# First two token groups routed inside the first attention, and GpSimd's scatters in fours

## The reference, cut to what matters

```python
x = x + tanh(g_xattn[0]) * L0_xattn(layernorm(x), ctx_1024, mask)      # 375 keys for each batch
h = layernorm(x)
# L0_ffn: mixture of 8 experts, top 2, 1024 places for each expert
probs = softmax(h @ Wr)                       # [3584, 8]
w_topk, e_topk = top_k(probs, 2)
pos = running count of the tokens of the same expert      # in the order of the tokens
buf[e, pos] = h                               # kept while pos < 1024
buf_out = expert_e(rms(buf)) + buf
y = h + sum_k w_topk[k] * buf_out[e_topk[k], pos[k]]      # where both of a token's places were kept
y = gelu(fh @ fWg) * (fh @ fWu) @ fWd + h                 # where one overflowed; fh = rms(h) * f_norm
x = x + tanh(g_ffn[0]) * y
```

## Time and profile before

| | us |
|---|---|
| median of three runs | 3190.02 (3184.22 to 3192.74) |
| profiled execution, first to last instruction | 3224.8 |
| first attention, up to the first instruction of the next block | 209.5 |
| routing stage, up to the last instruction on VectorE | 350.6 |
| busy over the span: TensorE, VectorE, ScalarE, GpSimd | 3044.6, 2015.2, 1460.1, 620.4 |

### The profile page before, as it was taken

The page is one execution under the profiler, slowest core; times in us unless marked ns, Lnnn a source line. Parts: engine busy times, 40 slices in busy tenths (PEclk is TensorE's granted clock), DMA queues, the critical chain, the costliest instruction groups (busy, mean ns, idle before and its releaser), DMA issues. The chain is left out here.

```text
span 3224.8 us, 61178 instructions
## 1 busy us (share of the span) xinstructions
PE 3044.6 (94%) x23544; PEld 2321.0 (72%) x23544; DVE 2015.2 (62%) x4390; ACT 1460.1 (45%) x2835; POOL 620.4 (19%) x895
## 2 busy tenths in 40 slices
PE   8995799997989999999999999799999999899999
PEld 6874456656779999999999999566666666566443
DVE  3454211125767777788787877566666666688654
ACT  3431111114645555555555555366666666455000
POOL 3535200024300013023002300112212111035000
PEclk8987899988999999999999999899999999999999
DMA  8652232236700000000000000000000000245000
GB/s 240 192 169 62 62 118 103 93 113 192 235 25 2 1 2 1 2 2 2 2 1 2 2 1 2 22 24 21 16 21 21 16 21 16 74 147 186 15 15 17
DMA packets 75072, 181.80 MB, mean 56 GB/s; under 512 B 12101, under 2 KB 18738, under 8 KB 74452
## 3 DMA queue, kind: packets, MB, share of 16 engines
q1 hardware_dynamic: 58260, 137.83, 13.5%
q10 hardware_dynamic: 10192, 25.30, 2.5%
q0 software_dynamic: 6336, 14.76, 1.6%
HBM read 150.25 MB, written 27.79 MB: 55 GB/s over the span
## 5 line engine op out<-in xcount | busy, mean ns | idle before, releaser
L2664 ACT ACTIVATE probs<-probs,neg_top 112x375 f32<-112x375 f32 x512 | 281.8, 599 | 12.8 <-DVE neg_top L2587 11.6
L2587 DVE CUSTOM_DVE_ANT_0 probs<-ps,add 112x375 f32<-112x375 f32 x512 | 250.2, 546 | 55.6 <-PE ps L2738 54.7
L3202 PE MATMUL ps<-we,xn_t 128*112 128x512 f32 x512 | 230.5, 614 | 0.9 <-PEq L736 0.9
L2144 DVE TENSOR_REDUCE top<-ps 112x16 f32<-112x1792 f32 x96 | 194.3, 2024 | 58.5 <-PE ps L2382 57.1
L2765 PE MATMUL ps<-ident,probs 112*125 112x112 f32 x1536 | 222.5, 281 | 2.8 <-DVE probs_t L2594 2.8
L2594 DVE COPY probs_t<-ps 125x336 f32<-125x336 f32 x256 | 128.9, 504 | 151.4 <-PE ps L2765 151.4
L1524 DVE TENSOR_TENSOR hidden<-gated,ps 128x512 f32<-128x512 f32 x64 | 44.0, 688 | 284.7 <-PE ps L1567 284.7
L2765 PEld LDWEIGHTS ps<-ident,probs 112*125 112x125 f32 x1536 | 189.7, 188 | 30.7 <-issue 18.9
L2160 DVE TENSOR_TENSOR probs<-probs,inv_sum 112x1792 f32<-112x1792 f32 x96 | 197.4, 2056 | 3.3
L2156 DVE TENSOR_REDUCE row_sum<-probs 112x16 f32<-112x1792 f32 x96 | 193.9, 2020 | 4.3 <-ACT probs L2268 4.3
L2148 DVE TENSOR_TENSOR probs<-ps,top 112x1792 f32<-112x1792 f32 x96 | 194.3, 2024 | 3.3
(11 more groups left out here) (419 smaller groups left out, 6255.2 us busy)
## 6 DMA issues: line engine op xcount, KB each, us to landing
ctx_t<-in_ctx_T_dram SPq DMA_DIRECT2D x96, 375.0 KB, 4.2
ctx_sb<-in_ctx_dram ACTq DMA_DIRECT2D x64, 384.0 KB, 5.7
ctx_sb<-in_ctx_dram SPq DMA_DIRECT2D x32, 384.0 KB, 6.0
ctx_sb<-in_ctx_T_dram SPq DMA_DIRECT2D x32, 375.0 KB, 3.0
queue<-zeros SPq DMA_DIRECT2D x32, 256.0 KB, 4.5
rows<-queue SPq DMA_DIRECT2D x16, 512.0 KB, 5.0
outputs<-out SPq DMA_DIRECT2D x16, 512.0 KB, 2.9
mask_in<-in_mask_BxSxS_fk_dram SPq DMA_DIRECT2D x16, 328.1 KB
```

The source lines that it names most:

```text
L2144: dve.tensor_reduce(top[:, :, :], scores, AX.X, ALU.max).then_inc(s["top_done"], 1)
L2587: dve.tensor_tensor_reduce(out=probs[:, u, h, :], in0=k.ps[0:S, SCORE + h, 0:L], in1=add[:, j % 2, :], scale=1.0, scalar=BIG, op0=ALU.add, ...
L2664: act.activation(probs[:, u, h, :], probs[:, u, h, :], ACT.Exp, bias=neg_top[:, u, h:h + 1], scale=-1.0).then_inc(s["probs_done"], 1)
L3202: mm = pe.matmul(k.ps[0:S, Y + at % YB, :], xn_t[:, j + u, c, :], r.we[:, c, e:e + TWO, :].rearrange("p e d -> p (e d)"), start=c == 0, st ...
```

## The change

The diff rewrites the routing as functions outside of the stages (`token_norm`, `token_shift`, `token_exp`, `token_pick`, `token_places`, `token_rows`, `token_scatter`, `token_gains`, `token_self`), whose bodies do what the functions above did, and calls them from two stages:

- Inside `first_attention`, from step 10 on, one batch is transposed and its logits computed in each step, 24 batches (three groups) in all. Groups 0 and 1 are routed completely: picked in steps 18 and 26, placed in steps 19 and 27, rows found in steps 20 and 28, and scattered two transfers to a step in steps 20 to 35. Group 2 is shifted and picked in step 34. `normalise` for 28 of 32 batches and `add_self` for 16 of them run there too. The block ends when the 32 scatters have landed.
- In `route_tokens` are left: the scales and norms of the last 4 batches, places and rows of group 2, all of group 3 but its first four norms, 32 scatters, and the whole shared branch, which has a new order. After every fourth scatter GpSimd waits until it has landed.
- The writes of zeros go out two to a step from step 5 on, so that all are out after step 20's load.
- The small tiles move into the memory of the network's weights, which is unused until `run_experts`; the scales are computed in halves of a group.

```diff
                     if j == CT:
                         sp.dma_start(k.x_sb[:, BODY:B, :], ...)
-                    else:
-                        sp.dma_start(fill[j - CT - 1], k.zeros[:, :]).then_inc(k.queue_zeroed, 16)
-                for n in range(B - CT - 1, B):
-                    sp.dma_start(fill[n], k.zeros[:, :]).then_inc(k.queue_zeroed, 16)
+                    for n in range(2 * (j - CT - 1), min(2 * (j - CT), k.zero_dmas)):
+                        if j > CT:
+                            sp.dma_start(fill[n], k.zeros[:, :]).then_inc(k.queue_zeroed, 16)
...
+                def scatter(j):                                   # GpSimd, first_attention
+                    g, turn = divmod(j - 20, G)
+                    if j == 20:
+                        pool.wait_ge(k.queue_zeroed, k.zero_dmas * 16)
+                    if 0 <= g < 2:
+                        for n in (2 * turn, 2 * turn + 1):
+                            token_scatter(k, t, pool, g, n)
...
+                token_half_scales(k, m, pool, 6)
+                for j in range(B, B + 4):
+                    pool.wait_ge(s["residual_done"], j - LAG)
+                    scatter(j)
+                for g in range(2):
+                    pool.wait_ge(t.scattered[g], 16 * G * TOP_K)
...
+                    if 0 <= j - TOKENS < ROUTED:                  # TensorE, first_attention
+                        transpose_token(j - TOKENS)
...
+                    if 0 <= j - TOKENS < ROUTED:
+                        token_logits(j - TOKENS)
+                    if 0 <= g < 2 and j == G * g + 19:
+                        token_places(k, m, t, pe, g, PLACES)
...
-                pool.wait_ge(k.queue_zeroed, k.zero_dmas * 16)    # GpSimd, route_tokens
-                for g in range(GROUPS):
-                    pool.wait_ge(s["put_ready"], g + 1)
-                    for j in range(G):
-                        for r in range(TOP_K):
-                            pool.indirect_dma_start(k.queue[:, :], ...).then_inc(scattered[g], 16)
+                token_half_scales(k, w, pool, GH * GROUPS - 1)
+                token_sizes(k, w, pool, LAST)
+                token_inverses(k, w, pool, LAST)
+                for g in (LAST - 1, LAST):
+                    for n in range(G * TOP_K):
+                        token_scatter(k, t, pool, g, n)
+                        if n % 4 == 3:
+                            pool.wait_ge(t.scattered[g], 16 * (n + 1))
...
+                for x in range(B - HB, B):                        # VectorE, route_tokens
+                    token_norm(k, w, t, dve, x)
+                token_rows(k, w, t, dve, LAST - 1, PLACES)
+                token_gains(k, w, t, dve, LAST - 1)
+                hide(0)
+                for x in range(G * (LAST - 1), G * LAST):
+                    token_self(k, t, dve, x)
+                hide(1)
+                token_shift(k, w, t, dve, LAST, LOGITS)
+                add_shared(0)
+                token_pick(k, w, t, dve, LAST)
+                hide(2)
+                add_shared(1)
+                token_rows(k, w, t, dve, LAST, PLACES)
+                hide(3)
+                token_gains(k, w, t, dve, LAST)
+                for x in range(G * LAST, B):
+                    token_self(k, t, dve, x)
+                add_shared(2)
+                hide(4)
+                for n in range(3, GH * GROUPS):
+                    add_shared(n)
+                    if n + 2 < GH * GROUPS:
+                        hide(n + 2)
...
+                token_places(k, w, t, pe, LAST - 1, PLACES)       # TensorE, route_tokens
+                gate_and_up(0)
+                for q in range(GH * DC):
+                    transpose(q)
+                gate_and_up(1)
+                for h in range(GH):
+                    route_rows(h)
+                down(0)
+                gate_and_up(2)
+                down(1)
+                gate_and_up(3)
+                token_places(k, w, t, pe, LAST, PLACES)
+                down(2)
+                for n in range(4, GH * GROUPS):
+                    gate_and_up(n)
+                    down(n - 1)
+                down(GH * GROUPS - 1)
```

More of the change, by code:

```diff
@@ L240, in first_attention @@
         QBK = 500
+        TOKENS, ROUTED = 10, 3 * G
+        XT = 256
+        LOGITS, PLACES = (k.ps[0:S, ATT, 256 + i * G * E:256 + (i + 1) * G * E] for i in range(2))
         GROUP = 4
@@ L1100, in mixture_weights @@
     w.coef = sb(nc, "coef", [S, TOP_K, B], F32)
-    names = "shared_loaded norms_loaded iota_ready tables_done gate_scaled up_scaled stats_done mean_done scale_step xr_scales_done r_invs_done"
+    names = ("shared_loaded norms_loaded iota_ready stats_done mean_done vars_scaled xr_scales_done sizes_done vars_shifted "
+             "token_rstd_done r_invs_done")
     w.s = {n: sem(nc, n) for n in names.split()}
-def token_scales(k, w, pool, g, part):
-    s = w.s
-    cut = slice(g * G, (g + 1) * G)
[L1109 to L1124, removed]
@@ new lines, in token_inverses, with routing_storage, piece @@
+def token_inverses(k, w, pool, g):
+    cut = slice(g * G, (g + 1) * G)
+    pool.wait_ge(w.s["vars_shifted"], g + 1)
+    pool.tensor_tensor(w.rstd[:, cut], w.var_eps[:, cut], k.neg_half[0:S, 0:G], ALU.pow).then_inc(w.s["token_rstd_done"], 1)
+    pool.wait_ge(w.s["token_rstd_done"], g + 1)
+    pool.tensor_tensor(w.r_inv[:, cut], w.r_inv[:, cut], w.rstd[:, cut], ALU.mult).then_inc(w.s["r_invs_done"], 1)
+def routing_storage(k, w, net):
+    nc = k.nc
+    t = Fields()
+    homes = (net.wq, net.wqh, net.wkh, net.wv)
+    t.xr = [home[0:S].rearrange("p n c d -> p (n c) d")[:, 0:G, :] for home in homes]
+    spare = net.wo[:, :, :, :].rearrange("p n c d -> p (n c d)")
+    rests = [home[:, :, :, :].rearrange("p n c d -> p (n c d)")[:, G * D:G * D + DC * HS] for home in homes]
+    rests += [spare[:, h * DC * HS:(h + 1) * DC * HS] for h in range(GH)]
+    t.xr_t = [rest.rearrange("p (c s) -> p c s", c=DC) for rest in rests]
+    taken = [GH * DC * HS]
+    def piece(*dims):
+        size = 1
+        for d in dims:
+            size *= d
+        at = spare[0:S, taken[0]:taken[0] + size]
+        taken[0] += size
+        if len(dims) == 1:
+            return at
+        names = "abcd"[:len(dims)]
+        return at.rearrange(f"p ({' '.join(names)}) -> p {' '.join(names)}", **dict(zip(names[1:], dims[1:])))
+    t.logits = piece(G, E)
+    t.top = piece(G)
+    t.exps = piece(G, E)
+    t.total = piece(G)
+    t.probs = piece(G, E)
+    t.best = piece(G, 8)
+    t.best_at = piece(G, 8).bitcast(U32)
+    t.best_f = piece(G, 8)
+    t.route = piece(TOP_K, G, E)
+    t.routes = piece(G, E)
+    t.group_count = piece(E)
+    t.place = piece(G, E)
+    t.late = piece(G, E)
+    t.picked = piece(2, TOP_K, G, E)
+    t.row_late = piece(2, TOP_K, G)
+    t.put_f = piece(TOP_K, G)
+    t.put_at = piece(B // G, TOP_K, G).bitcast(U32)
+    t.over = piece(G)
+    t.kept = piece(G)
+    t.shared_coef = piece(B // G, G)
+    t.coef_sum = piece(G)
+    t.self_gain = piece(G)
+    assert taken[0] <= NODES * DC * D
+    names = ("normed transposed xt_copied logits_done logits_taken logits_read exps_done routes_done places_done places_read dve_step put_ready self_added")
+    t.s = {n: sem(nc, n) for n in names.split()}
+    t.scattered = [sem(nc, f"scattered{g}") for g in range(B // G)]
+    t.steps = 0
+    return t
@@ new lines, in token_exp, with token_pick @@
+def token_exp(k, t, act, g):
+    act.wait_ge(t.s["logits_read"], g + 1)
+    act.activation(t.exps, t.logits, ACT.Exp).then_inc(t.s["exps_done"], 1)
+def token_pick(k, w, t, dve, g):
+    dve.wait_ge(t.s["exps_done"], g + 1)
+    linked(t, dve, dve.tensor_reduce(t.total, t.exps, AX.X, ALU.add))
+    linked(t, dve, dve.reciprocal(t.total, t.total))
+    linked(t, dve, dve.tensor_tensor(t.probs, t.exps, each(t.total, E), ALU.mult))
+    for j in range(G):
+        ins = dve.max(t.best[:, j, :], t.probs[:, j, :])
+    linked(t, dve, ins)
+    for j in range(G):
+        ins = dve.max_index(t.best_at[:, j, :], t.best[:, j, :], t.probs[:, j, :])
+    linked(t, dve, ins)
+    linked(t, dve, dve.tensor_copy(t.best_f, t.best_at))
+    for r in range(TOP_K):
+        ins = dve.tensor_tensor(t.route[:, r, :, :], w.iota[:, :].unsqueeze(1).broadcast_to([S, G, E]), each(t.best_f[:, :, r], E), ALU.is_equal)
+    linked(t, dve, ins)
+    dve.tensor_tensor(t.routes, t.route[:, 0, :, :], t.route[:, 1, :, :], ALU.add).then_inc(t.s["routes_done"], 1)
+    dve.wait_ge(t.s["routes_done"], g + 1)
+    dve.tensor_reduce(t.group_count, t.routes.rearrange("p g e -> p e g"), AX.X, ALU.add)
@@ new lines, in token_places @@
+def token_places(k, w, t, pe, g, at):
+    pe.wait_ge(t.s["routes_done"], g + 1)
+    if g:
+        pe.wait_ge(t.s["places_read"], g)
+    pe.matmul(at, k.tri[0:S, 0:S], t.routes.rearrange("p g e -> p (g e)"), start=True, stop=False)
```

(26 more changed lines are left out.)

369 lines of the change are left out of this document (179 added, 190 removed).

## The result

Before 3191.25 us, after 3176.11 us (medians of six runs each); the ratio is 0.9955, with an interval of 0.9943 to 0.9968. The change is 0.45% or about 15 us faster. The forecast was 3145 us with a range of 3127 to 3185. The sign is right and the time lies inside the range, but the gain was forecast at three times its size. 3176 is near what the first rival had said (3178, for late messages that the runs do not have) and what the third had said (3176, for long landings). Three single runs far above the rest of their kernel (7610.8, 5559.9 and 3240.9 us, all on one chip) are left out of the ratios.

What follows compares the result with a forecast made beforehand. TensorE was taken to bound the attention, a chain with GpSimd's scatters as spine the routing stage. 72 us gone in routing and 27 added in the attention make 45 less than the 3190 median: 3145 us, range 3127 to 3185.

Steps and rivals of the forecast that it cites:

- the first rival: Routing stage: late messages belong to the profiled execution alone; 12 us less, 3178 us; chance 0.24.
- the third: Routing stage: waits for landing cost what the gathers show, 31 us more, stage 100 us, time 3176; chance 0.07.
- Part 1, the attention: First attention: TensorE is full, so added work adds time, 27 us (18 to 40).
- The zero writes: First attention: zero writes going out twice as fast cost 2 us (0 to 5).
- The end of the block: End of first attention: later pick, last two scatters and their landing cost 7 us (3 to 10).
- Part 2, the new routing stage: Routing stage: GpSimd is the spine with 32 scatters for 64; the stage takes 69 us (60 to 85).
- the upper bound that the gathers gave: Routing stage: landing of a scatter, taken as 2.2 us, could take up to 6.7 us.
- The 6 us put in for waits between queues: Routing stage: allowance of 6 us for queues in a new order, on top of 63 us.
- the sum: Whole kernel: 72 us gone from routing, 27 added in the attention, 45 us subtracted from the median of 3190.
- My own count of the late messages: Routing stage before: four bursts lose 37.6 us; without that the stage would end near 314 in place of 350.6.
- the bound of the attention: Rival, first attention: GpSimd's scatters beside VectorE take over 1.65 us each and set the pace, making it slower; chance 0.08.
- theories C and D: Set up during the experiments: waits after fours keep late messages away on any chip (C); such a chip stays slower (D).

Runs made afterwards that it cites:

- e1: The kernel before, without an edit, traced a second time: 3187.91 us, its routing stage 111.7 us.
- e7: The kernel before with only the new order of the zero writes, two to a step, on the second chip: 3225.45 us, ratio 1.0015.
- the eights: The changed kernel with a wait after every eighth scatter in place of every fourth: 3167.94 us, ratio 0.9926.
- e6: e5 with all 64 scatters issued in the routing stage, on the second chip: 3225.89 us, ratio 1.0007.
- e5: The changed kernel without waits after fours, the wait for the first 32 landings moved to the routing stage's end, second chip: 3188.11 us, ratio 0.9893.
- e8: e5 with the pick of group 2 after VectorE's last residual, on the second chip: 3190.16 us, ratio 0.9884.

## Why the prediction was wrong

**Part 1, the attention, was right.** The start of the routing stage moved from 207.6 (e1) to 231.8, 24 us for 27, but that has the luck of the two openings in it. From the fourth mask instruction on, where the opening no longer counts, the way to the routing stage is this:

```profile
43.59 0.55 DVE L355 CUSTOM_DVE_ANT_0 probs<-ps,add 112x375 f32<-112x375 f32 x1 [1.89 <-PE ps L517]
```

```profile
41.47 0.55 DVE L375 CUSTOM_DVE_ANT_0 probs<-ps,add 112x375 f32<-112x375 f32 x1 [1.88 <-PE ps L561]
```

The first is e1, 207.6 - 43.6 = 164.0 us, the second the changed kernel, 231.8 - 41.5 = 190.3: 26.3 us, where the terms without the zero writes said 24.8. Of these terms, 24 steps at 0.60 us are 14.4 as forecast, `token_places` about 2 us each for 1.7, and pick left TensorE 99.73 of 100 us busy. The zero writes, 4.8 us (0.3 to 9) by e7 for 2, stay uncertain. The end of the block: VectorE ends at 223.90, the next block starts 7.9 us later where it was 2.5.

**Part 2, the new routing stage, was right:** 69.6 us for 69, fours of 7.07 for 7, with the first landing at 5.14 us near the upper bound that the gathers gave. The last few us are luck. The 6 us put in for waits between queues were not spent on these: GpSimd never waited for the rows of group 3. They went into two longer landings (3.6 us) and into the end of the block, 5.1 us after the last scatter.

**The step that failed is the sum:** "141.1 - 69 = 72 us gone", subtracted from the median. 141.1 us is the stage in one execution, with late messages that, by e1, the runs behind the median do not have. Where the kernel before takes 3188 us, the stage takes 111.7 us (e1), 29.4 less. So 42 us go, less 26 in the attention: 16 us, near the 15 measured. My own count of the late messages, 37.6 us, was too high as well: it adds up waits, and without them the stage does not end at 314 - 209.5 = 104.5 us but at 111.7. The sign that the trace and the runs were not of one kind was on the page, 34.8 us of span above the median, and the rival weighed it: but I gave it 0.24, and the forecast 0.55.

**The rivals.** "The late messages belong to the profiled execution alone" gave the right time, 3178: the runs behind the median do not have them, as it said. Its mechanism did not hold as put, for they are not the property of one profiled execution: they come back in four traces of one chip, where 22 runs of the kernel before take 3222 us at the median, nearly the span of the trace of before. That chip's traced runs lie within 3 us of the median of their kernels, and span and time of a run agree within about 2 us. The rule of the Trainium skill that I named beside it ("NOTIFIC — the notification-queue block", 7.1), that the unit which writes trace records can hold an engine back, stays open: each run here comes with its span, so none shows the kernel unrecorded. That the fours buy nothing and cost came out as that rival said: 9.5 us for the 14 of my estimate. GpSimd did not become the bound of the attention: its scatters beside VectorE take 0.94 to 1.28 us, where the price would begin at 1.65. So the rule of the Trainium skill ("SBUF — State Buffer", "SBUF: two separate sides"), that GpSimd can't write descriptors while VectorE holds the port that they share, showed no price here; whether VectorE ever held that port in these steps no run shows. Long landings, the third rival, gave 3176 by another road: 2 of the 7 waits inside the groups were longer than 2.4 us, by 2.8 and 0.9 us, and not 7 by 4.5. Whether late messages come back under fours is the question of theories C and D, and open.

## What to carry to other kernels

When a profiled span stands over 1% above the median of the runs, look for what the profile has and the runs lack before any sum is made, and subtract it from both sides. Waits that name no cause ("remote") are the first suspects. And trace the kernel before a second time: e1 alone would have shown the 29 us. This stage, whose spine is one engine issuing transfers, got shorter only by what left that engine: half of the scatters, not the computing around them. And a wait that is put in against an effect is paid also where the effect is absent: here 9 us for the fours, and for the eights 2 us by the medians, too little to be told from nothing.

## What the hardware showed that I had not expected

In the one session on the second chip, messages between engines came late during bursts of GpSimd's scatters. In its four traces the waits so named begin from 5.7 us after the start of a burst on; most last one to 14 us, the longest 27.8 (ScalarE in e6). Many end 1 to 3 us after the last scatter of their burst, but some end inside it. On the three other chips no trace of these kernels shows one. The kernel before took 3222 us on the second chip and 3188 to 3193 elsewhere. The 32 scatters inside the attention met none in e5 and e8, though not all go out in twos: GpSimd falls behind at the end of the block, and in e8 the last eight go out back to back (216.5 to 226.4). Whether the length of a burst alone brings the late messages, and what is different about that chip or that hour, is open.
